# A third PSUM bank for the up products, taken from the attention

## What is computed

```
x = x + ssm(layernorm(x))          # conv, silu, a scan over the 512 tokens
x = x + ffn(layernorm(x))          # 8 experts, 128 -> 512 -> 128, all of them, mixed by gates
x = x + attention(layernorm(x))    # 16 heads of 8, a local mask: own chunk of 10, 25 to the left
x = x + ffn(layernorm(x))          # the same weights again

g = x @ w_gate[e];  u = x @ w_up[e];  h = silu(g) * u
out = sum over e of (h @ w_down[e]) * cw[:, e]
```

## Time and profile before

| | us |
|---|---|
| median of 3 runs | 1482.62 (1482.54 to 1482.89) |
| the profiled execution, its own time | 1479.0 |
| its span | 1477.2 |
| TensorE busy, matmuls | 1406.2 (95%) |
| VectorE busy | 962.5 (65%) |
| ScalarE busy | 774.5 (52%) |
| GpSimd busy | 577.0 (39%) |
| TensorE's granted clock, mean | 0.99 of full speed |

### The profile page before, as it was taken

One profiled execution on the slowest core, in us unless ns is written; L12 is line 12 of the kernel. 1 busy time (PEld: TensorE's weight loads), 2 busy tenths in 40 slices (PEclk: granted clock), 3 DMA queues, 4 the chain that ended last, 5 costly groups with the idle time before them and its releaser, 6 DMA issues.

```text
span 1477.2 us, 27207 instructions
## 1 busy us (share of the span) xinstructions
PE 1406.2 (95%) x10580; PEld 1211.1 (82%) x10580; DVE 962.5 (65%) x2197; ACT 774.5 (52%) x1037; POOL 577.0 (39%) x513
## 2 busy tenths in 40 slices
PE   5698999999899999999999999999999999999998
PEld 3587878888788888787888878888888888888887
DVE  5656677665866667668675776757755666576543
ACT  6364738652566545646466474555644454355321
POOL 4351555533534454146531772147603531352000
PEclk9799999999999999999999999999999999999999
DMA  5120351004210420134003500062004200510000
GB/s 175 49 59 15 92 135 31 16 15 122 40 38 23 136 40 2 44 104 80 8 2 101 125 1 9 7 162 59 2 1 122 40 2 1 143 19 1 1 8 8
DMA packets 82860, 75.23 MB, mean 51 GB/s; under 512 B 5532, under 2 KB 60860, under 8 KB 82732
## 3 DMA queue, kind: packets, MB, share of 16 engines
q1 hardware_dynamic: 82732, 73.50, 19.2%
HBM read 60.65 MB, written 12.83 MB: 50 GB/s over the span
## 4 chain that ended last, share of the span: by engine, by line
PE 74%; DVE 10%; issue 5%; POOL 4%; ACT 4%; DMA 1%; SPq 1%; DVEq 0%; POOLq 0%; ACTq 0%
PE pd L1020 25%; PE pg L274 7%; PE pu L274 7%; PE pu L275 6%; PE pu L276 6%; PE pg L276 6%; PE pg L275 6%; PE att_ps L679 3%; DVE h L1113 2%; PE att_ps L701 1%; POOL arena L630 1%; DVE x L1101 1%; POOL arena L632 1%; DVE arena L583 1%; PE side_ps L311 1%
## 5 line engine op out<-in xcount | busy, mean ns | idle before, releaser
L1075 ACT ACTIVATE h<-pg 128x512 f32<-128x512 f32 x512 | 304.8, 599 | 637.4 <-PE pg L276 635.2
L1020 PEld LDWEIGHTS pd<-w_down,h 128*128 128x128 f32 x4096 | 510.0, 191 | 31.9 <-issue 3.5
L1020 PE MATMUL pd<-w_down,h 128*128 128x128 f32 x4096 | 524.7, 276 | 1.1 <-DVE x L1101 0.9
L1113 DVE TENSOR_TENSOR h<-h,pu 128x512 f32<-128x512 f32 x512 | 344.4, 678 | 207.9 <-PE pu L276 198.2
L274 PE MATMUL pg<-ffn_x_hi,w_gate_hi 128*128 128x512 f32 x512 | 243.8, 476 | 1.5 <-DVE ffn_x_lo L357 1.5
L274 PE MATMUL pu<-ffn_x_hi,w_up_hi 128*128 128x512 f32 x512 | 205.5, 401 | 18.0 <-DVE h L1113 17.6
L275 PE MATMUL pu<-ffn_x_lo,w_up_hi 128*128 128x512 f32 x512 | 203.2, 397 | 0.0
L276 PE MATMUL pg<-ffn_x_hi,w_gate_lo 128*128 128x512 f32 x512 | 203.0, 397 | 0.0
L275 PE MATMUL pg<-ffn_x_lo,w_gate_hi 128*128 128x512 f32 x512 | 203.0, 397 | 0.0
L276 PE MATMUL pu<-ffn_x_hi,w_up_lo 128*128 128x512 f32 x512 | 202.6, 396 | 0.0
L890 POOL TENSOR_TENSOR q_weights<-q,pack 128x512 fp32r<-128x512 f32 x136 | 142.9, 1072 | 74.0 <-DMA k<-qk_rows 74.0
(11 more groups left out here) (190 smaller groups left out, 1555.5 us busy)
## 6 DMA issues: line engine op xcount, KB each, us to landing
arena<-bc_spread SPq DMA_DIRECT2D x56, 256.0 KB, 4.7
att_arena<-v_rows SPq DMA_DIRECT2D x64, 144.0 KB, 3.9
qk_rows<-qk_parts SPq DMA_DIRECT2D x32, 256.0 KB, 2.3
q<-qk_rows SPq DMA_DIRECT2D x32, 256.0 KB, 3.6
k<-qk_rows SPq DMA_DIRECT2D x32, 256.0 KB, 4.5
att_arena<-v_rows SPq DMA_DIRECT2D x64, 128.0 KB, 3.4
arena<-in_x SPq DMA_DIRECT2D x8, 256.0 KB, 2.9
x<-in_x SPq DMA_DIRECT2D x8, 256.0 KB, 3.4
```

The costliest lines, as they stand in the source:

```text
L1020: last = nc.tensor.matmul(pd[:, t * P:(t + 1) * P], h_b[:, d % NH, t * P:(t + 1) * P], wd[:, d % NCH, :], start=d % CPE == 0 and t == 0, s ...
L1075: nc.scalar.activation(h_b[:, c % NH, :], pg[c % 2][:, :], ACT.Silu).then_inc(gate_done, 1)
L1113: nc.vector.tensor_tensor(h, h, pu[d % 2][:, :], ALU.mult).then_inc(h_done, 1)
```

## The change

`pu` gets three banks (`NU` = 3), so that up product d waits for the product with h of chunk d - 3. `att_ps` keeps one bank, through which all products of the attention go in turn: ln3, q, k, v, scores 0, scores 1, values 0, scores 2, values 1, and so on. Scores n + 2 thereby wait until VectorE has copied out values n. The projections are spread: k comes 1.5 chunks later than q, v 1.5 chunks later than before, with the pieces of ScalarE, VectorE and SP that belong to them. The values are due at n + 15/8 units instead of n + 7/4. In the first batch's scan, which borrows banks, the third `pu` bank takes the place of the second `att_ps`. Lines of the changed kernel are one higher than before.

```diff
--- before.py
+++ after.py
@@ -37,6 +37,7 @@
 SETUP = 40
 NXB = 4
 NH = 8
+NU = 3
 
 
 T_HEAD = [-4.5, 25] + [NCH * m - 8 for m in range(2, NM)]
@@ -179,9 +180,9 @@
         k3 = sb("k3", [P, 4, NKEY], F32R)
 
         pg = [ctx.enter_context(nc.psum_tensor(f"pg{i}", [P, L], F32)) for i in range(2)]
-        pu = [ctx.enter_context(nc.psum_tensor(f"pu{i}", [P, L], F32)) for i in range(2)]
+        pu = [ctx.enter_context(nc.psum_tensor(f"pu{i}", [P, L], F32)) for i in range(NU)]
         pd = ctx.enter_context(nc.psum_tensor("pd", [P, L], F32))
-        att_ps = [ctx.enter_context(nc.psum_tensor(f"att_ps{i}", [P, L], F32)) for i in range(2)]
+        att_ps = [ctx.enter_context(nc.psum_tensor("att_ps", [P, L], F32))]
         side_ps = [ctx.enter_context(nc.psum_tensor("side_ps", [P, L], F32))]
 
         packed, raw_loaded, stored = sem("packed"), sem("raw_loaded"), sem("stored")
@@ -194,7 +195,7 @@
         b_used, dx_done = sem("b_used"), sem("dx_done")
         g_full, u_full, gate_done, h_done = sem("g_full"), sem("u_full"), sem("gate_done"), sem("h_done")
         down_done, summed = sem("down_done"), sem("summed")
-        att_full, att_free = ([sem(f"att_{v}{i}") for i in range(2)] for v in ("full", "free"))
+        att_full, att_free = [sem("att_full")], [sem("att_free")]
         side_full, side_free = [sem("side_full")], [sem("side_free")]
         ln_sems = {k: (sem(f"{k}_stats"), sem(f"{k}_rstd"), sem(f"{k}_rows")) for k in ("ssm_ln", "att_ln", "ffn_ln")}
         fx_hi, fx_f32, route_exp, mix_ready = sem("fx_hi"), sem("fx_f32"), sem("route_exp"), sem("mix_ready")
@@ -268,7 +269,7 @@
         b = Banks(side_ps, side_full, side_free)
 
 
-        b_ps, c_ps = (pg[0], pg[1], pd, att_ps[1]), (pu[0], pu[1], att_ps[0], pg[0])
+        b_ps, c_ps = (pg[0], pg[1], pd, pu[2]), (pu[0], pu[1], att_ps[0], pg[0])
 
         def split3(out, w, x_parts, first=True, last=True):
             nc.tensor.matmul(out, w[0], x_parts[0], start=first, stop=False)
@@ -657,12 +658,12 @@
                 at, t0 = (lambda n: Att.at(j, n)), T_ATT[j]
                 yield t0 + 4
                 norm_pe(pe, ab, "att_ln", j, ("ln3", j), xn_att)
-                yield t0 + 6
-                ab.wait_free(pe, ("ln3", j))
                 for w, name in ((wq, ("q", j)), (wk, ("k", j))):
+                    yield t0 + (6 if w is wq else 7.5)
+                    ab.wait_free(pe, ("ln3", j))
                     ps = ab.take(pe, name)
                     ab.fill(split3(ps[:, :], [v[:, :] for v in w], (axh[:, 0:L], axl[:, 0:L])), name)
-                yield t0 + 7.5
+                yield t0 + 9
                 ps = ab.take(pe, ("v", j))
                 for t in range(TT):
                     out, xw = ps[:, t * P:(t + 1) * P], [a[:, t * P:(t + 1) * P] for a in (axh, axl)]
@@ -688,7 +689,7 @@
                     if n + 1 < NUNIT:
                         yield at(n + 1 + 1 / 8)
                         scores(n + 1)
-                    yield at(n + 1 + 3 / 4)
+                    yield at(n + 1 + 0.875)
                     if n in (0, NW // 4):
                         pe.wait_ge(v_set, 4 * j + (4 if n else 2))
                     name = ("o", j, n)
@@ -717,8 +718,8 @@
                 yield t0 + 4.5
                 ab.wait(act, ("ln3", j))
                 nc.scalar.copy(axh[:, 0:L], ab.ps(("ln3", j))[:, :]).then_inc(x_hi, 1)
-                yield t0 + 6.5
                 for w, v in enumerate("qk"):
+                    yield t0 + 6.5 + 1.5 * w
                     ab.wait(act, (v, j))
                     nc.scalar.activation(qk_s[:, w, 0, :], ab.ps((v, j))[:, :], ACT.Identity,
                                          bias=pk("b_" + v)).then_inc(qk_hi, 1)
@@ -740,12 +741,12 @@
                 dve.wait_ge(x_hi, j + 1)
                 ab.free(nc.vector.tensor_tensor(axl[:, 0:L], ab.ps(("ln3", j))[:, :], axh[:, 0:L].bitcast(F32),
                                                ALU.subtract), ("ln3", j))
-                yield t0 + 7
                 for w, v in enumerate("qk"):
+                    yield t0 + 7 + 1.5 * w
                     dve.wait_ge(qk_hi, 2 * j + w + 1)
                     ab.free(nc.vector.scalar_tensor_tensor(qk_s[:, w, 1, :], ab.ps((v, j))[:, :], pk("b_" + v),
                                                            qk_s[:, w, 0, :].bitcast(F32), ALU.add, ALU.subtract), (v, j))
-                yield t0 + 8
+                yield t0 + 9.5
                 ab.wait(dve, ("v", j))
                 if j == 0:
                     dve.wait_ge(v_pad, 32)
@@ -831,13 +832,13 @@
                     sp.wait_ge(qk_moved, 16 * 8 * (j - 1))
                 for w, v in enumerate("qk"):
                     for part in range(2):
-                        yield T_ATT[j] + 7 + 0.5 * w
+                        yield T_ATT[j] + 7 + 1.5 * w
                         if part == 0:
                             sp.wait_ge(qk_hi, 2 * j + w + 1)
                         else:
                             ab.wait_free(sp, (v, j))
                         sp.dma_start(qk_r[w, part], qk_s[:, w, part, :].bitcast(F32)).then_inc(qk_out[w][part], 16)
-                yield T_ATT[j] + 8
+                yield T_ATT[j] + 9
                 for w, (dst, parts) in enumerate(((q3, (0, 0, 1, 1)), (k3, (0, 1, 0, 1)))):
                     for i, part in enumerate(parts):
                         sp.wait_ge(qk_out[w][part], 16 * (j + 1))
@@ -845,7 +846,7 @@
                         sp.dma_start(dst[i::4, :, at0:at0 + L].bitcast(F32),
                                      qk_r[w, part].rearrange("(g e) l -> e g l", g=4)).then_inc(qk_moved, 16)
 
-                yield T_ATT[j] + 9
+                yield T_ATT[j] + 10
                 if j:
                     sp.wait_ge(v_moved[1], 16 * 8 * j)
                 ab.wait_free(sp, ("v", j))
@@ -1006,9 +1007,9 @@
                     d = c - 1
                     if 0 <= d < NC:
                         m = d // NCH
-                        if d >= 2:
-                            pe.wait_ge(h_done, d - 1)
-                        split3(pu[d % 2][:, :], [w[:, d % NCH, :] for w in wu],
+                        if d >= NU:
+                            pe.wait_ge(h_done, d - NU + 1)
+                        split3(pu[d % NU][:, :], [w[:, d % NCH, :] for w in wu],
                                (fxh[m % 2][:, :], fxl[m % 2][:, :])).then_inc(u_full, 1)
                     yield
                     for d in downs(c):
@@ -1110,7 +1111,7 @@
                         h = h_b[:, d % NH, :]
                         dve.wait_ge(gate_done, d + 1)
                         dve.wait_ge(u_full, d + 1)
-                        nc.vector.tensor_tensor(h, h, pu[d % 2][:, :], ALU.mult).then_inc(h_done, 1)
+                        nc.vector.tensor_tensor(h, h, pu[d % NU][:, :], ALU.mult).then_inc(h_done, 1)
                     d = c - 1 - LAG
                     if d >= 0 and d % CPE == CPE - 1:
                         weigh(d // CPE)
```

## The result

| | before | after |
|---|---|---|
| median of the runs | 1482.76 us (4 runs beside it) | 1504.39 us (4 runs, 1494.39 to 1506.47) |
| ratio, 95% interval | | 1.0131 [1.0086, 1.0177] |
| span of the profiled execution | 1477.2 us | 1504.7 us |
| TensorE busy | 1406.2 us | 1425.0 us |
| TensorE idle (span less busy) | 71.0 us | 79.7 us |

The account below looks back on a forecast made before the run. TensorE, busy 1406.2 of 1477.2 us, was taken as the bound, with only its idle time changing. Terms -8.0 - 2.1 + 16.8 + 2.6 = +9.3 us gave 1491.9 us, range for all 1476 to 1500.

Parts of the forecast that it names:

- The third up bank: Up products' 17.6 us of waits for the product with h go; other waits take some back, leaving 8.0 us gained.
- The values later: Values come a half step later on TensorE, so 2.1 of their 3.0 us of waits go.
- The scores behind the copy: Scores n+2 wait on the single attention bank for VectorE's copy of values n: 16.8 us lost.
- 14 to 18 in 15 to 20: Sign in the profile after: scores waiting for the values' copy, 14 to 18 us in 15 to 20 places.
- my 16 late places: Of 56 places, those where the copy ended after the scores' start in the kernel before, together 17.9 us.
- the 4.1 that three of these places take over from the up product: At 869.8, 1015.2 and 1062.2 scores wait instead of the up product, taking 4.1 us off the bank's gain.
- The projections: Spread q, k, v products: k waits 2.1 us more for q's bank, v 0.5 for k's; 2.6 us lost.
- I cost it at nothing: Later q and k reads delay GpSimd's query weights: costed at nothing; without cover up to 1 us at each of eight batches.
- TensorE's idle time rises from 71 to 80 us with the same busy time: Sign for the profile after: idle time up to 80 us, no change in TensorE's busy time.
- The copies come in time: Faster rival: copies about 1.1 us earlier at late places, scores' wait some 2 us, 1477 us; chance 0.17.
- Even: Rival: stalls let VectorE and ScalarE catch up, about half of 16.8 us returns, +1 us, 1483.5; chance 0.12.
- Worse: Rival: nine places with 0.6 or 0.7 us margin turn late and k reads arrive late, 1499.6 us; chance 0.10.

Follow-up runs that it names:

- Two pairs of runs: Three up banks against two: with banks shared by attention and side work, ratios 0.9938 and 1.0009; in the changed kernel, 1.0131 and 1.0203.
- The second probe: Kernel before with seven TensorE waits put in by hand, two ahead of batch 6 scores, two in batch 7, three in the tail; single run 1525.42 us.

## Why the prediction was right and wrong

- **The third up bank, -8.0 us.** The mechanism held: 17.6 us of waits went, and L1102 rose by 3.5 us (0.9 to 4.4) where I had 4.0. The values wait 3.5 us in 3 places, two of them the ones that I had named here for 1.5 us together; they took 1.1 and 2.2. Two pairs of runs put the bank's worth at 10.5 and 10.7 us. That is no more than their noise above 8.0; fewer waits and with them less time at 1.2 GHz would raise it.
- **The values later, -2.1 us.** Wrong, though small. The waits that I had counted went, but alone the later values moved the time by nothing: the up bank's waits rose by 2.0 us in their place, which I hadn't counted.
- **The scores behind the copy, +16.8 us.** The mechanism held, at the places where I had put it, for the same reason (sums, reciprocal and addition ahead of the copy). 18.1 us in 13 places were measured, for 14 to 18 in 15 to 20. Twelve of the 13 are among my 16 late places; of the other four, two wait 0.11 and 0.15 us and two not at all. The thirteenth is new, at 1023 us. By my own terms the line should have come to 20.9 us, 16.8 and the 4.1 that three of these places take over from the up product, so "14 to 18" was set too low for its working. The rule of the Trainium skill that the prediction cites (Perfetto Trace Analysis, Matmuls) was right in its direction; taken to say that every scores product pays, it overstates: 13 places pay and 43 don't. This term alone moved the time by 18.2 us, and in its trace idle time rose by only 10.9.
- **The projections, +2.6 us.** Together k and v waited 4.2 us for a bank, where 1.7 (before) and 2.6 make 4.3: right in the sum. The parts were not: k waited 2.7 us in 3 places, for 3 to 4, and v 1.5 in one, for 0.5. "I cost it at nothing", of the later reads of q and k, was wrong: with the v rows behind them they cost 4.3 us by themselves. I had looked only at the scores as those who wait for GpSimd's query weights, and not at what stands behind the query weights in GpSimd's own queue, the scan.
- **"TensorE's idle time rises from 71 to 80 us with the same busy time".** The first half came out at 79.7. The second half is the step that failed, and nearly the whole of the miss: in the profiled pair busy time rose by 18.8 us, by TensorE's clock, and in a typical pair by some 11 (the estimate above). The new wait alone raised it by 10.3 us. The kernel before showed the effect twice (the earlier trace rows is one: a wait of 1.63 us at 1015.2, with 1.2 GHz behind it), and I had priced a microsecond of waiting at a microsecond everywhere. The run in which the changed kernel's clock fell least, 1494.39 us, is within 3 us of the forecast.
- **The rivals.** Neither the faster nor the even one happened. "The copies come in time" names the right lever, though: with the copy made early, the time is that of before (1.0005), not the 5.5 us below it that I had worked out. "Even" put half of the scores' term as returning; 18.1 us of 20.9 stood. "Worse" came nearest in time, but not by its mechanism: the nine places with a margin of 0.6 or 0.7 us kept it in the changed kernel.

## What to carry to other kernels

When a change trades one wait of TensorE for another, compare the lengths and not the sums alone: in these traces every wait of 2.8 us or more had a stretch at half the clock with it or behind it (33 cases at eleven places), and of those from 0.9 to 1.4 us one in eleven. A PSUM bank taken away from a consumer has to be looked for on the engine that empties it: here a copy of 0.17 us, two instructions too late in VectorE's order, stood behind a wait that cost 18 us, and moving it brought back 16 to 19 us, where the bank is worth some 10. And a transfer moved later must be followed through the queue of the engine that waits for it, to the work that stands behind the wait.

## What the runs showed that I had not expected

- Time at 1.2 GHz is a cost of its own. The second probe adds 28.1 us of waits to the kernel before (19.4 for its memsets ahead of up products and 8.7 ahead of scores), and its span grew by 46.4 us; the stream's time at 1.2 GHz is 51.2 us against 6.8.
- Single waits of up to 2.77 us in the tail left the clock alone, and waits of 1.4 to 1.9 us in the stream had 1.2 GHz with them in 28 of 105 cases.
- One bank more for the up products, won by sharing two banks between the attention and the side work, is 0.6% of this kernel, with no change of order at all.
